# Expert phase of a fused attention and mixture-of-experts kernel: two tiles in flight against four

## What is computed

```python
x = x + xattn(ctx, layernorm(x), mask, ...)
tokens = layernorm(x).reshape(-1, 256)
topk_idx, topk_w = route(tokens)              # 4 of 32 experts a token
hidden = silu(tokens @ gate_w[e].T) * (tokens @ up_w[e].T)   # e of the 4, width 128
mixed = sum over the 4 of topk_w * (hidden @ down_w[e].T)
x = x + mixed + shared_expert(tokens)
```

## Time and profile before

| What | us |
|---|---|
| Median of 3 runs (1468.48 to 1471.33) | 1469.01 |
| The profiled execution, its own time | 1469.3 |
| Its span, from first to last instruction | 1467.3 |
| PE busy | 1349.2 (92%) |
| ACT busy | 1039.0 (71%) |
| DVE busy | 963.9 (66%) |
| POOL busy | 609.2 (42%) |
| Expert phase, 779 to 1317 us of the span: PE busy | 475.0 |

### The profile page before, as it was taken

How to read it: one execution, slowest core, us unless ns; L and a number is a source line. 1 busy time by engine, 2 the same in 40 slices (tenths; PEclk the granted TensorE clock), 3 DMA queues, 4 the chain that set the end, 5 groups by cost and what they waited for, 6 DMA issues and landing times.

```text
span 1467.3 us, 33057 instructions
## 1 busy us (share of the span) xinstructions
PE 1349.2 (92%) x8730; PEld 1050.3 (72%) x8730; DVE 963.9 (66%) x4500; ACT 1039.0 (71%) x2861; POOL 609.2 (42%) x662
## 2 busy tenths in 40 slices
PE   7999999999999999997778889888888889889997
PEld 4666666676666666665567778778778788778886
DVE  5578888888888888886653444444444444446788
ACT  5999999999999999996314655555555555553332
POOL 1004444444445444544442555555555555450000
PEclk8999999999999999999799999999999999999999
DMA  7145445544554455436735445444444444318886
GB/s 264 65 142 189 159 156 186 175 145 150 177 176 136 160 178 166 138 139 233 288 123 170 140 141 149 143 144 139 146 138 146 145 142 139 116 38 324 293 298 231
DMA packets 145780, 246.78 MB, mean 168 GB/s; under 512 B 22075, under 2 KB 108477, under 8 KB 145088
## 3 DMA queue, kind: packets, MB, share of 16 engines
q1 hardware_dynamic: 119488, 177.25, 37.4%
q0 software_dynamic: 26112, 67.42, 13.2%
HBM read 104.30 MB, written 120.09 MB: 153 GB/s over the span
## 4 chain that ended last, share of the span: by engine, by line
PE 55%; ACT 30%; issue 8%; DVE 4%; DMA 1%; another core or an unknown queue 1%; SPq 0%; ACTq 0%; DVEq 0%
PE ps L932 10%; PE psT L932 9%; PE psS L942 9%; ACT arena L1065 6%; PE ps L816 5%; ACT arena L1073 5%; PE ps L923 4%; PE psS L827 3%; ACT arena L1081 2%; ACT arena L1033 2%; PE ps L657 2%; PE psT L816 2%; ACT arena L1037 2%; ACT arena L988 2%; ACT arena L1025 1%
## 5 line engine op out<-in xcount | busy, mean ns | idle before, releaser
L601 POOL DMA_INDIRECT expert_out<-pay,dest x288 | 283.3, 984 | 277.3 <-DVE pay L1778 134.9
L544 POOL DMA_INDIRECT lists<-pay,slot x168 | 171.2, 1019 | 214.9 <-PE psT L727 39.5
L942 PE MATMUL psS<-arena,history 128*128 x576 | 182.0, 398 | 56.8 <-DVE history L1771 36.6
L1778 DVE TENSOR_SCALAR pay<-psS,dest 128x256 f32<-128x256 f32 x288 | 138.7, 481 | 76.7 <-PE psS L942 72.5
L932 PEld LDWEIGHTS ps<-pad,hist_j 128*128 128x128 f32 x1152 | 151.3, 194 | 16.4 <-ACT pad L1225 6.9
L932 PE MATMUL ps<-pad,hist_j 128*128 128x128 f32 x1152 | 155.7, 279 | 3.8 <-ACT pad L1225 3.7
L932 PEld LDWEIGHTS psT<-pad 128*128 128x128 f32 x1152 | 150.5, 193 | 11.4 <-issue 1.5
L932 PE MATMUL psT<-pad 128*128 128x128 f32 x1152 | 154.2, 277 | 0.5 <-ACT pad L1225 0.5
L942 PEld LDWEIGHTS psS<-arena,history 128*128 128x128 f32 x576 | 87.6, 192 | 74.3 <-issue 73.4
L544 POOL DMA_INDIRECT lists<-arena,slot x88 | 89.7, 1019 | 99.6 <-PE psT L727 19.7
L657 PE MATMUL ps<-arena 128*128 128x512 f32 x256 | 127.3, 620 | 2.1 <-ACT arena L1025 1.9
(11 more groups left out here) (238 smaller groups left out, 3334.8 us busy)
## 6 DMA issues: line engine op xcount, KB each, us to landing
lists<-pad SPq DMA_DIRECT2D x72, 516.0 KB, 6.7
pay<-lists SPq DMA_DIRECT2D x288, 129.0 KB
arena<-expert_out SPq DMA_DIRECT2D x32, 1024.0 KB, 6.9
pay<-pay SPq DMA_DIRECT2D x42, 384.0 KB
x<-in_x SPq DMA_DIRECT2D x32, 256.0 KB
out<-arena SPq DMA_DIRECT2D x32, 256.0 KB, 5.4
arena<-arena SPq DMA_DIRECT2D x20, 384.0 KB
arena<-in_ctx SPq DMA_DIRECT2D x32, 192.0 KB
```

The costliest lines, as they stand in the source:

```text
L544: pool.indirect_dma_start(lists, bass.IndirectOffsetOnAxis(ap=slots(u)[:, j, k:k + 1], axis=0), paid(u)[:, j, k, :], None).then_inc(scat[3 ...
L601: pool.indirect_dma_start(expert_out, bass.IndirectOffsetOnAxis(ap=dest[:, t % DESTS, 1:2], axis=0), yy[n], None, bounds_check=T * TOPK - ...
L942: pe.matmul(dbank[n % 2][:, 0:D], hh[:, n % 4, :], w_dn[:, at(e, 1), :].rearrange("p a n -> p (a n)"), start=True, stop=True)\
L1778: dve.tensor_scalar(yy[n], dbank[n % 2][:, 0:D], dest[:, t % DESTS, 0:1].bitcast(fp32), None, ALU.mult)\
```

## The change

Four tiles are in flight instead of two. There are four buffers for weight copies, four for turned rows and four gate-up banks (`ps2`, `ps3`, `ps4`, `psO`). The two banks for the transposes, the two down banks, the eight slots and the four places of `hh` stay. Turned rows and weight copies are made four tiles ahead (`AHEAD`), and the down projection and `weigh_result` follow the gate-up of three tiles later (`BEHIND`). To make room, Silu now writes into `hh` itself, and DVE multiplies there in place; the mask row and the bias row of the attention stage are declared wider, and serve as weight buffers in the expert phase. Each engine has the same instructions per tile as before.

```diff
+AHEAD = 4
+BEHIND = 3
...
-        xsT = flat_p[:, 0:2 * D].rearrange("p (b n) -> p b n", b=2)
-        w_now = [flat_p[:, 2 * D:4 * D].rearrange("p (k n) -> p k n", k=2),
-                 hist_j[:, :].bitcast(fp32).rearrange("p (k n) -> p k n", k=2)]
-        sg = flat_h[:, 0:4 * I].rearrange("p (b n) -> p b n", b=4)
-        hh = flat_h[:, 4 * I:8 * I].rearrange("p (b n) -> p b n", b=4)
+        hh = flat_h[:, 0:4 * I].rearrange("p (b n) -> p b n", b=4)
+        xsT = [flat_p[:, 0:D], flat_p[:, D:2 * D], flat_h[:, 4 * I:6 * I], flat_h[:, 6 * I:8 * I]]
+        w_now = [v.rearrange("p (k n) -> p k n", k=2)
+                 for v in (hist_j[:, :].bitcast(fp32), flat_p[:, 2 * D:4 * D],
+                           mask_row_all.rearrange("p a j n -> p (a j n)").bitcast(fp32), bo_mask[:, :])]
+        gu_bank = [ps[2], ps[3], ps[4], psO]
...
             def gate_up(t, n):
                 pe.wait_ge(xst_ev, t + 1)
                 pe.wait_ge(w_ready, t + 1)
-                ge(pe, hh_done, t - 1)
+                ge(pe, hh_done, t - 3)
...
-            turn_x(0, 0)
-            turn_x(1, 1)
-            for t in range(TILES + 1):
+            for t in range(AHEAD):
+                turn_x(t, t)
+            for t in range(TILES + BEHIND):
                 if t < TILES:
                     gate_up(t, t % SLOTS)
                     read_expert(t)
-                if t + 2 < TILES:
-                    turn_x(t + 2, (t + 2) % SLOTS)
-                if t >= 1:
-                    down_proj(t - 1, (t - 1) % SLOTS, expert[t - 1])
+                if t + AHEAD < TILES:
+                    turn_x(t + AHEAD, (t + AHEAD) % SLOTS)
+                if t >= BEHIND:
+                    down_proj(t - BEHIND, (t - BEHIND) % SLOTS, expert[t - BEHIND])
...
-                ge(act, gu_full, t - 1)
-                act.activation(xsT[:, n % 2, :], ps[n % 2][:, 0:D], ACT.Copy).then_inc(xst_ev, 1)
+                ge(act, gu_full, t - 3)
+                act.activation(xsT[n % 4], ps[n % 2][:, 0:D], ACT.Copy).then_inc(xst_ev, 1)
...
                 act.wait_ge(gu_full, t + 1)
-                ge(act, hh_done, t - 3)
-                act.activation(sg[:, n % 4, :], ps[2 + n % 2][:, 0:P], ACT.Silu).then_inc(sg_done, 1)
+                ge(act, dn_full, t - 3)
+                act.activation(hh[:, n % 4, :], gu_bank[n % 4][:, 0:P], ACT.Silu).then_inc(sg_done, 1)
...
                 dve.wait_ge(sg_done, t + 1)
-                ge(dve, dn_full, t - 3)
-                dve.tensor_tensor(hh[:, n % 4, :], sg[:, n % 4, :], ps[2 + n % 2][:, P:2 * P], ALU.mult)\
+                dve.tensor_tensor(hh[:, n % 4, :], hh[:, n % 4, :], gu_bank[n % 4][:, P:2 * P], ALU.mult)\
                    .then_inc(hh_done, 1)
```

More of the change, by code:

```diff
@@ L158, in build @@
         pay = sb("pay", [P, 4, TOPK, ROW])
[L159 to L160 removed]
+        mask_row_all = sb("mask_row", [P, 2, 2, 2 * P], bf16)
+        mask_row = mask_row_all[0:DH + 1]
+        bo_mask = sb("bo_mask", [P, 2 * D])
+        bo_b = bo_mask[:, 0:D]
+        mask_u8 = bo_mask[0:DH + 1, D:2 * D].bitcast(u8).rearrange("p (a j n) -> p a j n", a=4, j=2)
         ones_sq = sb("ones_sq", [P, P], bf16)
@@ L928, in gate_up @@
                 pe.wait_ge(w_ready, t + 1)
-                ge(pe, hh_done, t - 1)
+                ge(pe, hh_done, t - 3)
                 for which in range(2):
                     for k in range(2):
-                        m = pe.matmul(ps[2 + n % 2][:, which * P:(which + 1) * P],
-                                      w_now[1 - n % 2][:, k, which * I:(which + 1) * I],
-                                      xsT[:, n % 2, k * P:(k + 1) * P], start=k == 0, stop=k == 1)
+                        m = pe.matmul(gu_bank[n % 4][:, which * P:(which + 1) * P],
+                                      w_now[n % 4][:, k, which * I:(which + 1) * I],
+                                      xsT[n % 4][:, k * P:(k + 1) * P], start=k == 0, stop=k == 1)
                 m.then_inc(gu_full, 1)
@@ L944, in down_proj @@
                   .then_inc(dn_full, 1)
-            expert_regs = [pe.alloc_register(f"expert{d}") for d in range(4)]
+            expert_regs = [pe.alloc_register(f"expert{d}") for d in range(AHEAD)]
             expert = {}
             def read_expert(t):
-                reg = expert_regs[t % 4]
+                reg = expert_regs[t % AHEAD]
                 pe.load(reg, tab[0:1, t:t + 1])
                 expert[t] = pe.snap(reg, min_val=0, max_val=E - 1)
-            turn_x(0, 0)
-            turn_x(1, 1)
-            for t in range(TILES + 1):
+            for t in range(AHEAD):
+                turn_x(t, t)
+            for t in range(TILES + BEHIND):
                 if t < TILES:
@@ L1223, in rows_copy @@
                     act.wait_ge(sd_full, 2 * EARLY)
-                ge(act, gu_full, t - 1)
-                act.activation(xsT[:, n % 2, :], ps[n % 2][:, 0:D], ACT.Copy).then_inc(xst_ev, 1)
+                ge(act, gu_full, t - 3)
+                act.activation(xsT[n % 4], ps[n % 2][:, 0:D], ACT.Copy).then_inc(xst_ev, 1)
             def weights_copy(t, n, e):
-                ge(act, gu_full, t - 1)
-                act.activation(w_now[1 - n % 2], w_gu[:, at(e, 1)].rearrange("p a k n -> p (a k) n"), ACT.Copy)\
+                ge(act, gu_full, t - 3)
+                act.activation(w_now[n % 4], w_gu[:, at(e, 1)].rearrange("p a k n -> p (a k) n"), ACT.Copy)\
                    .then_inc(w_ready, 1)
@@ L1784, in keep_dest @@
                 dve.tensor_copy(dest[:, t % DESTS, :], xs[n][:, D:ROW].bitcast(i32)).then_inc(dest_kept, 1)
-            for t in range(4):
+            for t in range(AHEAD):
                 keep_dest(t, t)
-            for t in range(TILES + 1):
+            for t in range(TILES + BEHIND):
                 if t < TILES:
                     hidden(t, t % SLOTS)
-                if t + 4 < TILES:
-                    keep_dest(t + 4, (t + 4) % SLOTS)
-                if t >= 1:
-                    weigh_result(t - 1, (t - 1) % SLOTS)
+                if t + AHEAD < TILES:
+                    keep_dest(t + AHEAD, (t + AHEAD) % SLOTS)
+                if t >= BEHIND:
+                    weigh_result(t - BEHIND, (t - BEHIND) % SLOTS)
             def sum_rows(v):
```

20 lines of the change are left out of this document (10 added, 10 removed).

## The result

The changed kernel takes **1490.76 us** (median of 4 runs, 1489.49 to 1492.32). The kernel before, run beside it, takes 1470.17 us (1468.48 to 1476.96). The ratio is 1.0132 with a 95% interval of 1.0098 to 1.0166: 20 us slower, where 25 us faster were forecast, and 11 us above the upper end of the range. A second measurement in another set of runs gave 1.0110 (1.0071 to 1.0149).

What follows compares the result with a forecast made beforehand. The prediction took PE's stalls on completions withheld during POOL's scatter groups as the bound. It summed 1469.3 - 27 (larger groups) + 1.5 (start) + 0.9 (end) = 1444.7, forecast 1444 us, range 1414 to 1480 us.

Steps and rivals of the forecast that it cites:

- What bounds the kernel: Expert phase: PE's work is 1.55 us a tile; late completions inside POOL's scatter groups stall it, some 92 of 538 us.
- How far PE may run: PE past a withheld completion: 3.10 us instead of 1.77, then stopped at `turn_x(t+6)`; a gain of 1.33 us.
- What that is worth: POOL's groups in the expert phase grow from 3.6 to about 4.5 tiles, saving 27 us; bounds none and 53 us.
- results trickle through: During the longer group's extra 1.1 us of withholding, some results still reach POOL, adding perhaps 0.3 tile to a group.
- PE's restart: After a stall PE waits for Silu, weight copy and row copy, 1.28 us instead of 0.75; 0.5 us later.
- DVE's part costs nothing on either side: DVE in the expert phase loses a wait and multiplies in place in SBUF with the same operands: 0 either way.
- The start: Start of the expert phase: four transposes now precede the first gate-up, delaying it; counted as 1.5 us lost.
- The end: End of the expert phase: two more down projections after the last gate-up; 0.9 us lost, bounds 0 and 2.6.
- Full cover: Rival: delays come from outside with their own length, so about 40 large stalls each save 1.33 us; 1418 us, chance 0.17.
- Nothing gained: Rival: a tile still costs 1.86 us, with longer stalls instead of more frequent ones; 1469 to 1472 us, chance 0.18.
- Slower by the clock: Rival: longer PE pauses drop its clock to half for 3.3 us; 1496 us, chance 0.21 shared with an unseen group dynamic.
- a group dynamic that I have not seen: Unspecified behaviour of POOL's scatter groups making the kernel slower; no size given, sharing the 0.21 with the clock rival.

Runs made afterwards that it cites:

- weigh_first_again: Changed kernel, but in each step DVE weighs the result of tile t-3 before multiplying tile t; 1439.9 us, ratio 0.988 to the kernel before.
- rows_first_again: Changed kernel, but ACT copies the turned rows of tile t+4 before the weights of tile t+4; 1470.54 us, ratio 1.011 to the kernel before.
- the plain pair: Kernel before and changed kernel, each with SP's plain DMAs to consecutive rows instead of POOL's scatters; 1382.58 and 1385.17 us, ratios 0.948 and 0.951.
- the paced one: Kernel before and changed kernel, POOL's scatter of tile t also waiting until t+3 (before) or t+5 (changed) gate-ups are known; 1437.95 and 1437.29 us.

## Why the prediction was wrong

**What bounds the kernel: right.** That POOL's scatters withhold PE's completions was a coincidence in the trace and is now shown for these scatters as a whole: with plain stores of SP in their place there are no such stalls, 5.2% less time, and 1.54 us a tile.

**How far PE may run: right.** The stop is `turn_x`, three gate-ups on, and the row copy ends it. The rows after show it as foretold.

**What that is worth: here the prediction failed.** It held the pause at 2.09 us and let the groups grow to 4.5 tiles, 64 in number. Measured are 72 groups and 2.58 us. The 8 groups too many are 8 x 2.09 = 17 us, and the longer pause is 72 x 0.49 = 35 us; together 52 us, which is more than the 27 us forecast. POOL's other waits came out 14 us lower than that sum has them (73.2 us against 224 x 0.39 = 87), and the scatters 1 us higher: -27 + 52 - 14 + 1 = +12 us, which is what the split at the gate-ups shows (+12.3).

The pause grew because **the news now comes 0.83 us behind the group's end, where it came 0.11 us ahead of it** (table above). The prediction let results trickle through while PE went on, and so kept the end of the group and the news together. But what PE does meanwhile is withheld with the rest, and POOL's group ends before the news. A second part of the pause is the way behind the news, and there it matters **at which instruction DVE stands**. DVE works in order, and the loop puts the product of tile t ahead of the weighing of t-3. DVE's waits in the phase say where it stands. These are those of the kernel before:

```profile
DVE history L1771 <- ACT history L1236: 139.3, 178, 3.5
DVE history L1771 <- issue: 85.3, 62, 2.8
DVE pay L1778 <- PE psS L942: 72.5, 71, 1.8
```

These are those of the changed kernel:

```profile
DVE history L1776 <- ACT history L1241: 274.2, 262, 4.1
DVE pay L1783 <- PE psS L947: 28.6, 51, 2.1
DVE history L1776 <- issue: 17.2, 17, 3.1
```

At the product DVE waits 291 us in all, before 225 us. At the weighing it waits 29 us, before 73 us. Such a wait at the weighing stands in the DVE timeline of the kernel before, inside the group of the earlier trace rows:

```profile
818.64 0.49 DVE L1778 TENSOR_SCALAR pay<-psS,dest 128x256 f32<-128x256 f32 x1 [1.04 <-PE psS L942]
```

A result that came through late, but within the group, went straight to POOL and made its scatter of 819.96. Now DVE mostly stands at the product, with the weighings of older tiles behind it. These were not results that lay ready. The trace has the times of most semaphore updates, and in the 62 waits of DVE over 1.8 us at the product in which both are recorded, `dn_full` for the weighing never came ahead of `gu_full`; in 55 it came 0.09 us after it. So the order on DVE costs the way through Silu and product once the news is there, 0.49 us by the two stretches shown; 72 x 0.49 = 35 us is an estimate from them.

In the kernel before it costs nothing most of the time, since there `dn_full` comes 0.7 us or more after the news in 21 of 28 such waits, when the product is over. In the stretch of the earlier trace rows `gu_full` comes at 820.86 us, and `dn_full` for the down projection of 818.48 only at 821.64. `weigh_first_again` takes these 0.49 us out, keeps PE's reach, and turns the loss into a gain. It does not take out the later news, which still falls 0.45 us behind the group's end. PE's restart, which the prediction counted as a third of a step, does not seem to be in the cycle, by `rows_first_again`. The prediction's sentence that DVE's part costs nothing on either side was true of its instruction and left out its place.

**The start: somewhat less than counted.** Counted 1.5 us. From the transposes of tile 2 to the eleventh gate-up the changed kernel takes 0.8 us longer in the profiled pair (16.48 against 15.72), 0.1 in the plain pair and 0.9 in the paced one (801.98 - 784.90 against 800.79 - 784.63). The rest of the 3.4 us is a phase that began later in that execution.

**The end: mis-sized.** Counted 0.9 us with bounds 0 and 2.6, measured +3.3. With three weighings behind the last products POOL is left with a queue: its last eight scatters run 1.29 us apart.

**The rivals.** Full cover (1418) did not come: PE stands still longer than before (561 - 472 = 89 us against 63 us), and since there is no delay without the scatters, it does not come from outside with a length of its own. Nothing gained (1469 to 1472) expected longer stalls instead of more frequent ones; PE's stops are as long as before (1.24 us) and more frequent, 62 against 45, and the time rose. Slower by the clock (1496) is near in number and wrong in cause: the clock of the phase is 0.99, and PE's granted clock was not lower than in the earlier trace rows. The rule of the Trainium skill (TensorE: Matmul & The Clock Gate, What's actually happening) that the array is throttled by default and released by activity decided nothing here. The trace agrees with it in one place: after PE's wait of 4.23 us at the start of the phase the granted clock is 0.50 from 788.7 to 790.6 us. The 0.21 that the prediction gave to the clock "or a group dynamic that I have not seen" was for the second part of that phrase, and the range ended 11 us too low, because I priced only the clock there and not a longer pause.

**Open.** Why the scatters withhold PE's completions is not explained, nor why it happens in some sets only. Nor is it settled why the news comes later against the group's end when PE runs 3.10 us on, which is the root of the longer pause. I did not try the weighing first in the kernel before or with a lag of one, so it is not shown whether that order mends a fault of the depth or would help both. Other DMA forms on POOL were not tried either.

## What to carry to other kernels

When a completion can be late, look for the instruction at which each in-order engine will stand meanwhile, and put the work that the next engine waits for (here the weighing of an old tile, whose input came with the news) ahead of the work on the newest tile, which has a longer way to go. Deeper buffers lengthen what the producer may do, but not what the consumer gets, and a gain that rests on the length of a pause must price that pause again for the new order. Where an engine's bursts hold up the others, holding it back by a wait can be worth more than any depth.

## What the runs showed of the hardware

Matmul completions on PE reach ACT and DVE late while indirect DMAs of POOL follow one another at 1.29 us: by 2.45 and 3.13 us in the two stretches shown, and over 2 us after the modelled end of the gate-up at 49 of 288 Silus before and 130 after (ACT's own catching up is in these counts). When SP stores the tiles by plain DMAs, every Silu starts 0.04 us after that end (1382.6 against 1458.9 us). In the changed kernel the withheld completions come out together, in PE's order: `gu_full`, `xst_full` and `dn_full` at 820.79, 820.84 and 820.88 us. The Trainium skill (DMA: Bandwidth & Descriptors, SWDGE vs HWDGE vs iDMA) says that GpSimd writes the descriptors of its own DMAs itself into rings in SBUF, while those of SP are made by hardware and are immune to the interference from VectorE that it describes; the plain runs agree that SP's stores do not disturb the kernel, but a delay of TensorE's news is not in that rule, and no run here shows the interference that it means.

In these two kernels the lateness prefers two values. Of 66 idle times of ACT over 1.8 us in the changed kernel, 51 end 1.9 to 2.0 us after the start of the last scatter; of 43 in the kernel before, 24 end 0.9 to 1.0 us after it (counted from the timelines of both engines). The step between them is about one scatter, 0.98 us. It is no general rule: in `rows_first_again` only 6 of 69 such idle times end near either value.

The same program took 1365.7, 1453.9 and 1472.6 us in different sets, and 1458.9 and 1472.6 in the two sets on chip 15, so the chip alone does not tell. In the fastest set nothing was withheld from the variants that were profiled, and two of them that stand at 0.988 and 1.011 elsewhere both came out at 1.000: PE is at its 1.54 us a tile there whatever stands around it.
